# Graph network with four layers: pair counts in two-byte numbers against lane numbers in PSUM, and node block numbers that lie unpacked

## The reference

```python
edge_index = jnp.stack([src, dst])
x = _layernorm(x + _L0(x, edge_index, ...))   # attention, 4 heads: softmax over the edges of one src
x = _layernorm(x + _L1(x, mask, ...))         # sums over dst neighbours of each src, weighted by degree
x = _layernorm(x + _L2(x, edge_weight, edge_attr, ...))  # a product of features, radial net and direction, summed by dst
x = _layernorm(x + _L3(x, edge_index, ...))   # two graph convolutions with self loops, summed by dst
```

## Time and profile before

| | |
|---|---|
| median of 3 runs | 19856.78 us (19844.69 to 19869.48) |
| the profiled execution | 19880.46 us |
| its span | 19878.6 us |
| mean granted TensorE clock | 0.677 |
| VectorE busy | 16662.2 us (84%) |
| POOL busy | 13030.6 us (66%) |
| TensorE busy | 9075.4 us (46%) |
| ScalarE busy | 6250.4 us (31%) |

### The profile page before, as it was taken

The page is one execution under the profiler, slowest core; times in us unless marked ns, Lnnn a source line. Parts: engine busy times, 40 slices in busy tenths (PEclk is TensorE's granted clock), DMA queues, the critical chain, the costliest instruction groups (busy, mean ns, idle before and its releaser), DMA issues.

```text
span 19878.6 us, 288457 instructions
## 1 busy us (share of the span) xinstructions
PE 9075.4 (46%) x63545; PEld 6845.3 (34%) x63546; DVE 16662.2 (84%) x22374; ACT 6250.4 (31%) x13799; POOL 13030.6 (66%) x13651
## 2 busy tenths in 40 slices
PE   0114110110113777532347777887888864336432
PEld 0114010100113666432235555555555543225322
DVE  9989999999998888755659999999999976665666
ACT  0000233333332555220005555555555553004200
POOL 0048777777777777777757777777777613770476
PEclk9655555555557999555558998888888865555555
DMA  1023444444522222552331111111111165345534
GB/s 18 0 54 24 29 32 33 33 33 30 32 20 50 47 47 47 171 162 69 84 52 13 13 13 13 13 13 13 13 13 13 12 156 188 79 74 190 163 79 68
DMA packets 1751558, 1095.99 MB, mean 55 GB/s; under 512 B 1217323, under 2 KB 1658124, under 8 KB 1750028
## 3 DMA queue, kind: packets, MB, share of 16 engines
q0 software_dynamic: 454272, 412.11, 18.9%
q1 hardware_dynamic: 1089532, 417.46, 8.5%
q10 hardware_dynamic: 207632, 265.14, 4.2%
HBM read 700.94 MB, written 391.12 MB: 55 GB/s over the span
## 4 chain that ended last, share of the span: by engine, by line
POOL 33%; DVE 25%; issue 16%; DMA 13%; DVEq 7%; PE 5%; ACT 1%; POOLq 0%; SPq 0%; ACTq 0%
POOL gat L784 17%; POOL pay L750 12%; DVE red L2516 12%; DMA srcs<-spread,nbx 9%; DVE srcs L2509 5%; DVEq L2515 4%; POOL srcs L806 4%; DMA spread<-srcs 3%; PE banks L1272 3%; DVE arena L1733 2%; DVE srcs L2505 2%; ACT srcs L1016 1%; DVEq L1803 1%; DVEq L2499 1%; DVE g_s L2500 1%
## 5 line engine op out<-in xcount | busy, mean ns | idle before, releaser
L784 POOL DMA_INDIRECT gat<-tab,nbr x3328 | 3511.2, 1055 | 2150.4 <-DMA nbr<-nbr_src 1136.4
L806 POOL DMA_INDIRECT srcs<-spread,nbx x2808 | 2654.7, 945 | 2312.0 <-DMA nbx<-from_src 1375.6
L784 POOL DMA_INDIRECT gat<-tab,pay x3328 | 3172.1, 953 | 1083.7 <-issue 821.4
L1416 PE MATMUL banks<-w2rows,dsts 128*128 128x384 f32 x6656 | 3021.2, 591 | 928.9 <-DVE srcs L2509 739.1
L750 POOL DMA_INDIRECT pay<-records,nbr x2560 | 2523.7, 986 | 798.2 <-issue 779.6
L2516 DVE TENSOR_REDUCE red<-srcs 128x160 f32<-128x2560 f32 x832 | 2346.2, 2820 | 76.1
L1272 PE MATMUL banks<-srcs,hot 128*128 128x96 bf16 (+1 forms) x11232 | 1148.1, 278 | 2742.7 <-DMA srcs<-spread,nbx 2651.4
L1201 PE MATMUL banks<-ident,arena 128*128 128x128 f32 x2240 | 433.2, 380 | 4224.2 <-DVE arena L1761 2807.0
L902 ACT COPY banks<-arena 128x1024 f32<-128x1024 f32 (+1 forms) x1508 | 1323.6, 879 | 3300.8 <-DVE arena L1761 1274.8
L2200 DVE TENSOR_TENSOR arena<-arena,banks 128x96 f32 (+2 forms) x2816 | 723.1, 257 | 1449.0 <-PE banks L1272 1155.5
L1272 PEld LDWEIGHTS banks<-srcs,hot 128*128 128x128 bf16 x11232 | 875.2, 134 | 3015.7 <-issue 1594.9
(11 more groups left out here) (392 smaller groups left out, 20625.4 us busy)
## 6 DMA issues: line engine op xcount, KB each, us to landing
spread<-srcs SPq DMA_DIRECT2D x936, 192.0 KB
dsts<-key_rows SPq DMA_DIRECT2D x234, 512.0 KB
spread<-srcs ACTq DMA_DIRECT2D x468, 204.0 KB
staged<-gat SPq DMA_DIRECT2D x416, 148.0 KB, 1.8
gat<-staged ACTq DMA_DIRECT2D x416, 148.0 KB
dsts<-key_rows ACTq DMA_DIRECT2D x117, 512.0 KB
gat<-tab,nbr POOLq DMA_INDIRECT x3328
gat<-tab,pay POOLq DMA_INDIRECT x3328
```

The source lines that it names most:

```text
L784: pool.indirect_dma_start(out=gatv(s, GC[pas])[:, t, :], out_offset=None, in_=TAB[pas], in_offset=bass.IndirectOffsetOnAxis(ap=row, axis=0 ...
L806: pool.indirect_dma_start(out=chunk_rows(s, c)[:, q, :], out_offset=None, in_=rows, in_offset=bass.IndirectOffsetOnAxis(ap=nbx[:, r, s * X ...
L1416: last = t_.matmul(bank[1 + 2 * (p % 2) + h][:, 0:384], hid_rows[:, s % 2, 2 * p + h, :], w2rows[:, :], start=True, stop=True)
```

## The change

In `pair_counts` the compare gets the form of the attention's compare. The lane numbers are written to PSUM bank 5 as two-byte pairs ahead of the loop; `own_w` and `nbr_w` get one more column (set to -1 where 3125 is odd), the tiles are laid out `p t w q`, and TensorE reads every second value of a tile. The last step has 6 edges instead of 5.

The block numbers are no longer packed. Each of the four tables holds one number a group, in a row of its own of the tile `win_rows` (partitions 0, 32, 64 and 96). `pack_windows` goes away, and `group_windows` loads four neighbouring words into four registers.

```diff
-        own_w = acc[:, 0:(TE + 1) // 2].bitcast(BF16)[:, 0:TE]
-        nbr_w = acc[:, 1600:1600 + (TE + 1) // 2].bitcast(BF16)[:, 0:TE]
-        pair_hot = [[acc[:, ...].bitcast(BF16).rearrange("p (t w) -> p t w", w=W)
+        own_w = acc[:, 0:(TE + 1) // 2].bitcast(BF16)
+        nbr_w = acc[:, 1600:1600 + (TE + 1) // 2].bitcast(BF16)
+        pair_lanes = acc[:, 3400:3400 + P]
+        pair_hot = [[acc[:, ...].bitcast(BF16)
+                     .rearrange("p (t w q) -> p t w q", w=W, q=2) for k in range(2)] for b in range(2)]
...
+        win_rows = sb("win_rows", [97, NG], I32)
+        win_att, win_dst = win_rows[0:1, :], win_rows[32:33, :]
+        win_src, win_nbr = win_rows[64:65, 0:XG], win_rows[96:97, 0:XG]
...
         def group_windows(eng, which, win_tab, n):
-            _, (word,) = nc.values_load_multi_w_load_instructions(
-                win_tab[0:1, bass.ds(n, 1)], engines=(which,), ...)
-            fields = [((word >> (WIN_BITS * q)) & ((1 << WIN_BITS) - 1)).with_bounds(min_val=0, max_val=W - 1) for q in range(GPS)]
-            for field in fields:
-                eng.to_reg(field)
-            return fields
+            _, four = nc.values_load_multi_w_load_instructions(
+                win_tab[:, bass.ds(n * GPS, GPS)], engines=(which,), min_val=0, max_val=W - 1, ...)
+            return four
...
-                        mm = t_.matmul(bank[0][0:W, 0:W], pair_hot[b][0][:, t, :], pair_hot[b][1][:, t, :],
+                        mm = t_.matmul(bank[0][0:W, 0:W], pair_hot[b][0][:, t // 2, :, t % 2], pair_hot[b][1][:, t // 2, :, t % 2],
...
+                    v.memset(out_[:, TE:TE + TE % 2], -1.0)
...
+                v.tensor_copy(pair_lanes.bitcast(BF16).rearrange("p (n q) -> p n q", q=2),
+                              iota[:, :].rearrange("p (n a) -> p n a", a=1).to_broadcast([P, P, 2]))
+                dve.drain()
+                v.tensor_copy(bank[5][:, 0:P], pair_lanes)
+                dve.drain()
...
                         last = v.tensor_tensor(
-                            pair_hot[b][k][:, 0:tiles, :],
-                            iotaw.rearrange("p (a w) -> p a w", a=1).to_broadcast([P, tiles, W]),
-                            ends[:, bass.ds(n * HT, tiles)].rearrange("p (t a) -> p t a", a=1).to_broadcast([P, tiles, W]),
+                            pair_hot[b][k][:, 0:tiles // 2, :, :],
+                            lane_pairs[:, 0:W, :].rearrange("p (a w) q -> p a w q", a=1).to_broadcast([P, tiles // 2, W, 2]),
+                            ends[:, bass.ds(n * HT, tiles)].rearrange("p (t a q) -> p t a q", a=1, q=2).to_broadcast([P, tiles // 2, W, 2]),
                             ALU.is_equal)
...
-            def pack_windows(words):
-                fields = win_group[:, 0:GPS * words.shape[1]].rearrange("a (n q) -> a q n", q=GPS)
-                v.tensor_copy(words[:, :], fields[:, GPS - 1, :])
-                for q in range(GPS - 2, -1, -1):
-                    ...shift left by WIN_BITS, or the next field in
```

More of the change, by code:

```diff
@@ L32 @@
 GROUP = TILES_PER_GROUP * P
-WIN_BITS = 7
 SLOTS = 4
@@ L199, in resnorm_gnn_kernel @@
         hot = sb("hot", [P, 2, TPS, P])
-        own_w = acc[:, 0:(TE + 1) // 2].bitcast(BF16)[:, 0:TE]
-        nbr_w = acc[:, 1600:1600 + (TE + 1) // 2].bitcast(BF16)[:, 0:TE]
-        pair_hot = [[acc[:, 8192 + (2 * b + k) * 784:8192 + (2 * b + k + 1) * 784].bitcast(BF16).rearrange("p (t w) -> p t w", w=W)
-                     for k in range(2)] for b in range(2)]
+        own_w = acc[:, 0:(TE + 1) // 2].bitcast(BF16)
+        nbr_w = acc[:, 1600:1600 + (TE + 1) // 2].bitcast(BF16)
+        pair_lanes = acc[:, 3400:3400 + P]
+        pair_hot = [[acc[:, 8192 + (2 * b + k) * 784:8192 + (2 * b + k + 1) * 784].bitcast(BF16)
+                     .rearrange("p (t w q) -> p t w q", w=W, q=2) for k in range(2)] for b in range(2)]
         high_w = acc[:, 0:DGROUPS * DIGITS // 2].bitcast(BF16)
@@ L492, in group_windows @@
         def group_windows(eng, which, win_tab, n):
-            _, (word,) = nc.values_load_multi_w_load_instructions(
-                win_tab[0:1, bass.ds(n, 1)], engines=(which,), min_val=0, max_val=(1 << (WIN_BITS * GPS)) - 1,
-                skip_runtime_bounds_check_because="each field is clamped to W - 1 where the word is made")
-            fields = [((word >> (WIN_BITS * q)) & ((1 << WIN_BITS) - 1)).with_bounds(min_val=0, max_val=W - 1) for q in range(GPS)]
-            for field in fields:
-                eng.to_reg(field)
-            return fields
+            _, four = nc.values_load_multi_w_load_instructions(
+                win_tab[:, bass.ds(n * GPS, GPS)], engines=(which,), min_val=0, max_val=W - 1,
+                skip_runtime_bounds_check_because="each block number is clamped to W - 1 where it is made")
+            return four
         def sort_pairs(t, bit, low, up):
@@ L1152, in pair_counts @@
                     step(i * 2 + 2, 0, HT)
-                step(full, 1, TE % HT, last=True)
+                step(full, 1, TE % HT + TE % 2, last=True)
                 pe.wait_ge(pairs_kept, 1)
@@ L1571, in pair_counts @@
                     dve.drain()
-                    v.tensor_copy(out_, whole)
+                    v.tensor_copy(out_[:, 0:TE], whole)
+                    v.memset(out_[:, TE:TE + TE % 2], -1.0)
                     dve.drain()
+                v.tensor_copy(pair_lanes.bitcast(BF16).rearrange("p (n q) -> p n q", q=2),
[3 more added lines that the diff above has]
+                dve.drain()
                 def step(n, b, tiles):
@@ L1589, in pair_counts @@
                     step(i * 2 + 2, 0, HT)
-                step(full, 1, TE % HT)
+                step(full, 1, TE % HT + TE % 2)
                 dve.wait_ge(pairs_used, full + 3)
@@ L1637, in source_windows @@
                 for part in range(4):
-                    v.tensor_scalar(win_group[:, :].rearrange("a (k q) -> a q k", q=QROWS)[:, part * rows_:(part + 1) * rows_, :],
+                    v.tensor_scalar(win_att.rearrange("a (k q) -> a q k", q=QROWS)[:, part * rows_:(part + 1) * rows_, :],
                                     bank[part][0:1, 0:rows_ * BLOCKS].rearrange("a (q k) -> a q k", k=BLOCKS), float(W - 1), None, ALU.min)
                 dve.drain()
-                pack_windows(win_att)
             def window_tables():
@@ L1661, in window_tables @@
                 for words, parts in ((win_src, 2), (win_nbr, 2), (win_dst, 4)):
-                    q = GPS * words.shape[1] // parts
+                    q = words.shape[1] // parts
                     for part in range(parts):
-                        v.tensor_scalar(win_group[:, part * q:(part + 1) * q], bank[b][0:1, 0:q], float(W - 1), None, ALU.min)
+                        v.tensor_scalar(words[:, part * q:(part + 1) * q], bank[b][0:1, 0:q], float(W - 1), None, ALU.min)
                         b += 1
-                    dve.drain()
-                    pack_windows(words)
+                dve.drain()
             def insert(place, limit, key, wide):
```

5 lines of the change are left out of this document (removed).

## The result

| | median, us | runs, us | against the kernel before |
|---|---|---|---|
| before | 19859.51 | 19844.69 to 19869.48 (4 runs) | |
| changed | 19674.54 | 19673.63 to 19678.73 (4 runs) | ratio 0.9907, 95% interval 0.9892 to 0.9923 |

The change saves 185 us. The forecast was 19645 us, with a range from 19550 to 19785. The profiled spans differ by more, 19878.6 - 19673.4 = 205 us, since the profiled execution of before lies 21 us above its median.

The account below looks back on a forecast made before the run. POOL's run, not busier VectorE, was taken to bound the kernel up to the radial pass, which is VectorE's. Terms -177 - 5 - 30 = -212 us took the median 19857 to 19645 us, range 19550 to 19785.

Parts of the forecast that it names:

- POOL in the pair counts, -177: Pair counts: with lanes in PSUM, POOL's 391 issues go at 1.249 us each, 488 us in place of 665.
- VectorE's compare, worth 0: Pair counts: the compare shortens to 971 ns, saving VectorE some 320 us that only end in front of POOL.
- Packing, -5: Before POOL begins: dropping the first table's packing and the wait for a later load moves POOL up 5 us.
- Register loads: Each use: four neighbouring words loaded without ALU_OPs, in place of one word and seven ALU_OPs; counted only in later spread passes.
- The low end: Register loads: four words come in the time of one, 0.31 us, with 0.70 us saved per use.
- each of four words pays: Rival, second and third spread pass: each word costs a full load, 0.22 us a pair lost, +103, 19778 us; chance 0.10.
- Spread passes, -30: Second and third spread pass: less register work on TensorE gains 30 us, close to the store loop's limit.
- 1.15 to 1.20 us a step: Sign of being right: pace of the second and third spread pass, against 1.22 us a step before.
- The key load can go out a little earlier when TensorE is ahead: Second and third spread pass: reason for the 30 us, since each fourth store queues behind the key load.
- the loop of a store slot: Second and third spread pass: store and copy, 4.81 us per four steps, 1.20 a step, limiting the gain to 0 to -15.
- Radial pass, 0: Radial pass: saved register loads on TensorE and ScalarE are covered by other work, worth 0.
- over 2 us of cover: Radial pass: VectorE takes TensorE's first products over 2 us late; 92 us at stake if that cover were gone.

Follow-up runs that it names:

- kernel 2: The kernel before with the change's unpacked block numbers but the old compare; 19888.48 us, ratio 1.0007 to the kernel before.
- kernel 3: The changed kernel with the compare in its old form, each number once, four-byte lanes still read from PSUM; 19687.20 us, ratio 0.9905 to before.
- kernel 4: The changed kernel with the same lane pairs read from SBUF in place of PSUM; 19795.69 us, ratio 0.9957 to the kernel before.
- kernel 7: The changed kernel with TensorE's four numbers loaded by four one-word loads in the second and third spread pass; 20074.66 us, ratio 1.0100 to before.
- kernel 6: The changed kernel with each fourth step's store ahead of the key load in the second and third spread pass; 19679.82 us, ratio 0.9903 to before.
- kernel 1: The kernel before with only the new pair compare, block numbers still packed; 19758.58 us, ratio 0.9944 to the kernel before.
- kernel 8: New compare with packed numbers, plus six small matmuls in each radial step ahead of the sums; 19767.41 us, ratio 0.9943 to the kernel before.
- kernel 9: New compare with packed numbers, plus five empty instructions on TensorE, VectorE and ScalarE ahead of the radial loop; 19791.09 us, ratio 0.9961 to before.

## Why the prediction was right, step by step

- **POOL in the pair counts, -177.** Right in mechanism and size. Its gathers, first to last issue, take 180 us less; with 3 us in the records and 3 in the hand-over (18.27 to 15.26) and the packing this is the 194 us by which L801 starts earlier. Kernels 2, 3 and 4 show the mechanism.
- **VectorE's compare, worth 0.** 965 ns against 971 predicted; kernel 3 shows that its shortening is worth nothing once the lanes lie in PSUM.
- **Packing, -5.** POOL's first issue comes 7.7 us earlier in the changed kernel, 5.7 in kernel 2. The size of it cannot be told in the time.
- **Register loads.** The low end held: 333 ns for four words, 9 ns for each word after the first. The 200 ns a register that the prediction took from the Trainium skill (Runtime: NRT & Kernel Launch, section Instruction fetch mechanics) would have made it 0.91 us. No load here behaves so, and the Trainium skill need not be wrong: the same page, section Terms, has such a load fetch its registers from HBM, while these read SBUF. Of the rival "each of four words pays", kernel 7 shows what it would have cost: some 395 us, not 103, since its sum left out the address operation ahead of each load.
- **Spread passes, -30.** This term was mis-sized: it measured 0. The two passes take 1141 us against 1138 in the kernel before; over all kernels with the key load first, kernel 7 left aside, they take 1136 to 1142 with packed numbers and 1141 to 1152 with unpacked ones. The sign that the prediction named, 1.15 to 1.20 us a step, did not come: 1.22 in both. "The key load can go out a little earlier when TensorE is ahead" is the sentence that failed; in kernel 6 even the store ahead of it gains 6 us in the passes. The bound named in the same paragraph, the loop of a store slot, held. (The 221 pieces of issue read there are not one for each pair, since 400 steps are 200 pairs; they make 1.20 us a pair and not 1.08.)
- **Radial pass, 0.** Right in the changed kernel (5674 us against 5673). But "over 2 us of cover" was no safe ground: it looked at one step at TensorE's upper clock, and kernels 1, 8 and 9 show the same pass 80 to 110 us longer, with late steps where the clock stays down for 10 us or more. No term of the prediction says why the changed kernel is spared that; here it was lucky.

The sum, with 0 for the passes, is -182; the medians differ by 185 and the profiled spans by 205.

## What to carry to other kernels

When another engine's queue sets the time, look at what each engine's instructions do to that queue's pace, not at how long they take: here a compare of unchanged length let POOL finish 180 us earlier once one of its inputs lay in PSUM. Put neighbouring register values side by side and load them in one instruction. Test the parts of a change each alone and together: their gains need not add up, because a pass that nobody touched can change its rhythm.

## What the runs showed of the hardware that was not expected

- A compare with both inputs in SBUF delays POOL's indirect transfers more when its lanes are two-byte numbers than when they are four-byte ones: 1.78 us an issue (kernel 4) against 1.70 (kernel 2), with 1.25 undisturbed.
- Four neighbouring words from SBUF load in 333 ns on TensorE, 344 on VectorE, 309 on ScalarE; four separate loads take 1.84 us on TensorE.
- Matmuls whose stationary and moving operands both step over every second two-byte value take 1.57 us for 16 at a granted clock of 0.50, the same as contiguous ones at that clock, and 0.96 us at 1.00.
- The same radial pass, instruction for instruction, has 2 late steps in one kernel and 50 in another; TensorE's granted clock stands at 0.50 for 10 to 14 us at such steps. Matmuls in one of the two waits ahead of them did not keep it up; the other wait, of 1.6 us and more, was left.
